# Two adapter layers on one core: four VectorE operations of tile 2 moved behind a transpose

## The reference

```python
# layer 0: one low-rank adapter per sequence (rank 16), chosen by id
B_req = B[adapter_ids]; A_req = A[adapter_ids]
Bx  = einsum('bni,bri->bnr', x, B_req)
x   = x + einsum('bnr,bor->bno', Bx, A_req)
# layer 1: a dense weight, plus 8 experts (rank 16), the best two by row
base   = einsum('btd,od->bto', x, W)
logits = einsum('btd,ed->bte', x, Wr) + 5.0 * one_hot(language_ids)[:, None]
topw, topi = top_k(logits, 2)
gates  = sum(one_hot(topi) * softmax(topw)[..., None], axis=-2)
h      = einsum('btd,erd->bter', x, A)
x      = x + base + 2.0 * einsum('bter,bte,eor->bto', h, gates, B)
```

## Time and profile before

| | us |
|---|---|
| median of three executions | 539.65 |
| their range | 539.64 to 539.96 |
| the profiled execution, own time | 539.96 |
| its span, first to last instruction | 538.2 |
| TensorE busy | 527.5 (98%) |
| VectorE busy | 329.1 (61%) |
| ScalarE busy | 213.9 (40%) |
| GpSimd busy | 175.3 (33%) |

### The profile page before, as it was taken

How to read it: one execution, slowest core, us unless ns; L and a number is a source line. 1 busy time by engine, 2 the same in 40 slices (tenths; PEclk the granted TensorE clock), 3 DMA queues, 4 the chain that set the end, 5 groups by cost and what they waited for, 6 DMA issues and landing times.

```text
span 538.2 us, 9381 instructions
## 1 busy us (share of the span) xinstructions
PE 527.5 (98%) x3500; PEld 477.7 (89%) x3500; DVE 329.1 (61%) x829; ACT 213.9 (40%) x493; POOL 175.3 (33%) x162
## 2 busy tenths in 40 slices
PE   6899999999999999999999999999999999999997
PEld 5788899998889998889999888999888999988897
DVE  4788765756655665766565665666566656557421
ACT  3645443344433334444334443433444433344211
POOL 6462322334322233432233333223333223441100
PEclk9999999999999999999999999999999999999999
DMA  8933434344324344423434432434442343421101
GB/s 332 312 96 99 141 102 116 100 128 126 88 86 123 89 127 128 117 81 98 123 94 127 128 89 86 121 90 127 127 121 82 94 128 89 128 88 41 40 40 40
DMA packets 30865, 60.42 MB, mean 112 GB/s; under 512 B 4316, under 2 KB 20060, under 8 KB 30820
## 3 DMA queue, kind: packets, MB, share of 16 engines
q1 hardware_dynamic: 24144, 38.81, 23.8%
q0 software_dynamic: 6656, 20.98, 13.0%
q10 hardware_dynamic: 20, 0.03, 0.0%
HBM read 43.02 MB, written 16.78 MB: 111 GB/s over the span
## 4 chain that ended last, share of the span: by engine, by line
PE 94%; DVE 3%; ACT 1%; POOL 1%; issue 1%; DMA 0%; ACTq 0%
PE o_bank L453 75%; PE o_bank L467 8%; PE x_bank L372 5%; PE b_bank L354 3%; PE b_bank L342 1%; PE o_bank L442 1%; DVE w_lo L687 1%; DVE a_raw L730 1%; PE o_bank L342 0%; DMA ids<-in_itok_B_dram 0%; DVE top_no L792 0%; POOL a_in L258 0%; DVE lb_t L702 0%; DVE x_lo L687 0%; PE x_bank L419 0%
## 5 line engine op out<-in xcount | busy, mean ns | idle before, releaser
L453 PE MATMUL o_bank<-w_hi,x_hi 128*128 128x512 f32 (+1 forms) x744 | 259.3, 349 | 0.0
L453 PE MATMUL o_bank<-w_hi,x_lo 128*128 128x512 f32 (+1 forms) x744 | 252.4, 339 | 0.0
L453 PE MATMUL o_bank<-w_lo,x_hi 128*128 128x512 f32 (+1 forms) x744 | 251.8, 338 | 0.0
L283 POOL TENSOR_TENSOR a_t<-a_raw,a_t 64x1024 fp32r<-64x1024 f32 x30 | 72.2, 2407 | 285.6 <-ACT a_t L575 285.6
L453 PEld LDWEIGHTS o_bank<-w_hi,x_hi 128*128 128x128 f32 x744 | 140.0, 188 | 15.9 <-issue 5.8
L453 PEld LDWEIGHTS o_bank<-w_hi,x_lo 128*128 128x128 f32 x744 | 139.7, 188 | 11.0
L453 PEld LDWEIGHTS o_bank<-w_lo,x_hi 128*128 128x128 f32 x744 | 140.1, 188 | 9.9
L626 ACT COPY out_sb<-o_bank 128x324 f32<-128x324 f32 (+1 forms) x96 | 40.0, 446 | 216.7 <-PE o_bank L467 216.7
L258 POOL DMA_INDIRECT a_in<-in_L_cond_A_dram,a_run x64 | 63.5, 992 | 19.2 <-issue 19.2
L712 DVE STREAM_TRANSPOSE x_bank<-x_in 128x512 f32<-128x512 f32 x60 | 69.1, 1197 | 0.2
L730 DVE STREAM_TRANSPOSE a_raw<-a_in 128x1024 f32<-128x1024 f32 x32 | 65.2, 2039 | 0.0
(11 more groups left out here) (102 smaller groups left out, 438.8 us busy)
## 6 DMA issues: line engine op xcount, KB each, us to landing
out_dram<-out_sb SPq DMA_DIRECT2D x31, 512.0 KB, 2.6
x_in<-in_x_dram SPq DMA_DIRECT2D x120, 128.0 KB, 3.7
w_in<-in_L_cond_W_dram SPq DMA_DIRECT2D x6, 512.0 KB, 8.8
x_in<-in_x_dram SPq DMA_DIRECT2D x2, 512.0 KB, 3.3
out_sb<-in_L_cond_W_dram SPq DMA_DIRECT2D x2, 512.0 KB, 14.8
a_in<-in_L_cond_A_dram,a_run POOLq DMA_INDIRECT x64, 5.0
w_in<-in_L_cond_A_dram SPq DMA_DIRECT2D x1, 512.0 KB, 4.5
b_in<-in_L_cond_B_dram,b_run POOLq DMA_INDIRECT x32
```

The lines of the kernel that those rows point to most:

```text
L283: nc.gpsimd.tensor_tensor(lower, a_raw[Q:P, :], lower.bitcast(F32), ALU.subtract).then_inc(a_lo_ready, 1)
L453: mm = pe.matmul(O[part][:, 0:hi - lo], xs[:, n % 2, c, :], w[:, c, lo:hi], start=(k == 0), stop=(k == K3 - 1), skip_group_check=True)
```

## The change

In VectorE's stream at n = 1, bx_rest(2) moves from ahead of a_lo_part(2) and xT_part(3) to behind them. With that, n = 1 has the same order as all other n, but for a_lo_part(2), which VectorE does only there. No other line changes.

```diff
                 if n == 1:
-                    bx_rest(2)
                     a_lo_part(2)
-                    xT_part(3)
-                else:
-                    if n + 2 < T:
-                        xT_part(n + 2)
-                    if n + 1 < T:
-                        bx_rest(n + 1)
+                if n + 2 < T:
+                    xT_part(n + 2)
+                if n + 1 < T:
+                    bx_rest(n + 1)
                 choose_experts(n)
                 weigh_experts(n)
```

## The result

| | before | with the change |
|---|---|---|
| median, us | 539.64 | 544.80 |
| executions in it, us | 539.31 to 539.96 | 544.03 to 545.87 |
| ratio of the times | | 1.0099, 95% interval 1.0087 to 1.011 |

The change makes the kernel slower: the medians are 5.2 us apart. The ratio of 1.0099 takes in 19 more executions of the changed kernel; all 23 took between 544.03 and 546.04 us. The forecast was 542.8 with a range up to 544.7, so the sign held and the size did not. The extra 2 us are not in VectorE's new order. They are in TensorE's clock.

What follows compares the result with a forecast made beforehand. TensorE was taken to bound the kernel, at 94% of the chain. Its add_l0(2) load, at 53.50 instead of 50.30 us, adds 3.20 us to the median of 539.65: forecast 542.8 us, range 542.3 to 544.7.

Steps and rivals of the forecast that it cites:

- The bound, the wait and its owner: TensorE is 94% of the chain; in tile 1 its add_l0(2) waits for a_lo(2) and bx_t, losing 0.22 us.
- Steps 1 to 4: At n = 1: a_lo starts 48.72, transposes 49.97, bx_all 52.1 to 52.2; bx_t ready 53.35 to 53.45, TensorE's load 53.50.
- The term of 3.20 us: Delay of TensorE's add_l0(2) load by waiting for bx_t: 53.50 instead of 50.30, other ends 3.1 to 3.3 us.
- The whole rest of the kernel is the old one, nothing adds to it: Everything behind add_l0(2) only shifts by 3.2 us; nothing gives it back and nothing adds to it.
- The sign of being wrong: The forecast is wrong if tile 1 grows by less than 3 us, or any later tile has another length.
- Rival 1: TensorE's clock falls in the 3.1 us hole, up to 3.2 us more: 542.8 to 546.0, middle 544.4; chance 0.23.
- Its sign: L453 part 1 matmuls spaced wider than 0.15 us after 54.4, perhaps with a lower digit of the granted clock.
- Rival 2: TensorE runs make_part(1, 1) matmuls while add_l0(2) waits, covering the 3.2 us: 539.4; chance 0.02.
- Rival 3: The twice 0.2 us of "issue" waits per tile eat the delay within 8 tiles: 539.65; chance 0.02.

Runs made afterwards that it cites:

- e8: Kernel before with VectorE's order at n = 1 changed to xT_part(3), bx_rest(2), a_lo_part(2): 540.74 us against 539.79, ratio 1.0013.
- e2: Kernel before with VectorE's order at n = 1 changed to a_lo_part(2), bx_rest(2), xT_part(3): 540.88 us against 539.45, ratio 1.0020.
- e1: Changed kernel with 28 matmuls of 128 columns that contribute nothing, put on TensorE ahead of add_l0(2): 543.27 us, ratio to the kernel before 1.0061.
- e11: The kernel of e1 run again, in the series that also holds e10: 543.33 us, ratio to the kernel before 1.0060.
- e10: The changed kernel unaltered, run again on the same chip as e11: 544.86 us, ratio to the kernel before 1.0091.
- e9: Changed kernel with 7 matmuls of 512 columns ahead of add_l0(2), filling the first half of the hole: 543.85 us, ratio to the kernel before 1.0067.
- e3: Kernel before with VectorE's order at n = 1 changed to bx_rest(2), xT_part(3), a_lo_part(2): 543.27 us against 539.45, ratio 1.0070.
- e5: Changed kernel with 14 matmuls of 128 columns ahead of add_l0(2), filling the first half of the hole: 545.02 us, ratio to the kernel before 1.0101.
- e6: Kernel before with five VectorE operations of no use to the result ahead of bx_rest(15) in tile 14: 545.58 us against 539.79, ratio 1.0108.
- e7: Kernel before with nine VectorE operations of no use to the result ahead of bx_rest(15) in tile 14: 548.41 us, ratio 1.0156.

## Why the prediction missed

**The bound, the wait and its owner: right.** TensorE bounds the kernel, and add_l0(2) is where the change lands. From 67.27 us on nothing differs.

**Steps 1 to 4: right to 0.1 us.** With the 0.60 us by which tile 1 began late, the forecast puts a_lo at 49.32, the transposes at 50.57, bx_all at 52.7 to 52.8, the end of bx_t at 53.95 to 54.05 and the load at 54.10. The changed kernel's rows say 49.30, 50.55, 52.71, 53.62 + 0.35 = 53.97, and 54.03. The term of 3.20 us measured 3.1.

**"The whole rest of the kernel is the old one, nothing adds to it": wrong.** This is the step that failed. Behind the hole TensorE runs at half clock for a while, worth 1.5 to 2.9 us, which the sum had at nothing, and this is part of every execution of the changed kernel: none of the timed ones lies under 544.0, while the longest execution of the kernel before, 540.37, and the wait of 3.1 us make only 543.5. The sign of being wrong looked only for a tile 1 that grows by less than 3 us; it grew by 67.27 - 60.68 - 0.60 = 6.0. The rest did hold: the later tiles are 15.87 to 15.90 us long, gated was ready at 55.80 + 0.29 and TensorE turned it at 62.4, and x_lo moved with TensorE to 63.20.

**Rival 1: right in mechanism and in price, wrong in its chance.** It said 542.8 to 546.0 with 544.4 in the middle, from the slow matmuls at 10.00 and 15.31; the median is 544.8. Its sign showed, too: matmuls of L453 0.27 us apart and a lower digit of the granted clock. Its chance stood at 0.23, on the ground that a hole of 1.33 us had left the pace alone and that dense work stood on both sides. That row was asked to carry too much. It says that 1.33 us were harmless there, and e8 and e2, with holes of 0.7 and 0.9 us, don't contradict it. It says nothing on 3.1 us, more than twice as much. And dense work on both sides did not help; what helped was matmuls all through the hole (e1). Nor do the 1.56 us of idle at 10.00 explain the slow start: in the changed kernel's profile the same four transposes, behind 1.57 us of idle at 10.15, take 0.71 us, and slow matmuls come only later. So it is in part luck that a price taken from that stretch came out right. Since the trace had no longer hole with dense work on both sides, it left open which way 3.1 us would go, and the price was known. The likeliest case should have been the one with the fall, 544.4, and the range would have reached to 546.
The rule of the Trainium skill (TensorE: Matmul & The Clock Gate, Part 1: The HAM clock gate), half clock after idleness and full clock only after sustained work, is what the changed kernel's rows of the granted clock show, 0.50 from 55 to 59 us; I had weighed it against one row.

**Rival 2: ruled out.** No weights of L453 were loaded before bx_t was ready: the row at 55.69 follows the eight loads at 54.03, behind 3.52 us of idle. The Trainium skill's reorder window (TensorE: Matmul & The Clock Gate, Architectural detail) did not reach past the wait here.

**Rival 3: ruled out.** The total "issue" waits per tile are the same as before, and no later tile is shorter.

**The spread: too small.** I allowed 0.3 us from run to run, from three executions within 0.32 us. Nineteen executions of the kernel before in one series reach from 538.93 to 540.37. That alone would not have carried the median out of the range.

## What to carry to other kernels

When a change makes a busy TensorE wait, price the wait and then ask whether the clock survives it: a row that shows a shorter hole as harmless is no evidence for a longer one. On the engine that prepares its inputs, whatever lies in front of the last input counts in full, and the same two transposes in that engine's idle time (e8) cost 0.7 us. If a hole can't be avoided, matmuls that do nothing can be worth their issue (e11 gave back 1.5 us of the 4.9 that e10 lost).

## What the runs showed of the hardware

- Holes in front of a dense stream, by TensorE's own idle time, and the clock behind them. 0.7 us (e8) and 0.9 us (e2): it stayed in both profiles, and no execution but the one of 2910 us is longer, by more than 0.05 us, than the longest of the kernel before and the wait; a dip worth some 0.5 us (an estimate: 0.001 of 539 us) is not excluded, since the mean granted clock of four executions of e2 reads 0.996 where none of the kernel before does. 1.6 us behind wide filler (e9): three of six executions 2 us longer, one of them profiled. 2.1 us (e3): two of four longer by 1.3 us or more, unprofiled. 1.7 us behind narrow filler (e5) and 3.0 us or more (the changed kernel, e6, e7): all longer. The fall is in the granted clock of every profile of the last group.
- The clock can fall after work has begun again: at 55.3 us in e5 and e9 and at 261.4 us in e6, 1.4 to 1.5 us behind the end of the hole. In the changed kernel's first profile it fell about 0.5 us ahead of it.
- At the lower level matmuls of 324 columns start 0.27 us apart, against 0.15 us at full clock, and their weight loads take 0.33 us against 0.19. The eight matmuls of add_l0 take 1.97 us against 1.11.
- A fall cost 1.5 us or 2.9 us, whatever the length of the hole, 3.5 or 6.4 us at the load.
- The kernel before has two lengths. In the first series the five of 19 executions whose mean granted clock is recorded as 1.000 took 539.99 to 540.37 us, the 14 with 0.993 to 0.997 took 538.93 to 539.65. Where the 0.8 us arise is not shown, and the profiles don't place them ahead of tile 1: e2 and e3, whose record reads 0.58 to 0.74 from 10 to 20 us, begin tile 1 at 44.69 and 44.56, and the kernel before and e1, whose record reads 1.00 there, at 44.51 and 44.65.
- A full reading at the start of a trace is no proof of full clock. The 16 matmuls of make_bx take 1.08 us at 15.31 in the kernel before, where the record reads 1.00, and 1.08 us at 15.52 in e2, where it reads 0.50; later they take 0.64 us.
